# Softmax row sums inverted through 32x32 transposes, and one exponential of 128x1024 for both heads of a tile

## The chip, the cores and the metric

The kernel runs on one core of a Trainium2 chip. The metric is the device time of one execution in microseconds (us). A core has TensorE (PE in the profile; its weight loads are PEld), VectorE (DVE), ScalarE (ACT), GpSimd (POOL) and SyncE (SP, which only issues transfers here). Each engine runs its own instructions in order; they meet at semaphores.

## The reference

An image batch x of shape (8, 512, 32, 32) is group-normalised. A small gate (mean over the pixels, two layers, a sigmoid, a threshold) sends each channel to one of two branches. Both branches are multi-head self-attention over the 1024 pixels ("tokens") with 512 channels and 8 heads of 64. The first ("hyperbolic") branch scales every token before and after by functions of its norm. The result is x + branch 1 + branch 2. Cut to what the change touches, for each image and branch:

```
scores = einsum('bhnd,bhmd->bhnm', q, k) / sqrt(64)
attn = softmax(scores, axis=-1)
out = einsum('bhnm,bhmd->bhnd', attn, v)
out = out @ w_o + b_o
```

All data is float32. The softmax is computed here as exp(score - maximum), multiplied with v, and the product is multiplied at the end with 1 / (sum of the exponentials).

## The kernel before

The loops run over 8 images `i` and the 2 branches `t`, so there are 16 stages of some 239 us. A stage has 32 batches `b`, each of two score tiles. A score tile `g` holds 128 keys against 512 queries (half `h` of the tokens) for the two heads of a pair `p`; the heads lie in the two halves of the 128 partitions. `ph = 2p + h` counts the eight phases of a stage, each of 8 tiles (4 batches). The last stage of the last image is called "closing" in the code: nothing follows it, so work for the next image is left out.

TensorE (L1355 to L1536) works in a fixed order written out by hand. In a batch it makes the score tiles `scores(2b)`, `scores(2b+1)` (L1431, matmul L1449: a pair of matmuls, one for each head, in each of four terms), two tiles of scores of which only the maximum is wanted (`max_slot`, L1406, matmul L1413), the products with v of tiles already exponentiated (`prob_v`, L1454, matmul L1463), now and then the row sums (`denominator`, L1468, matmul L1477 with a matrix of ones), and a share of the next projections (`halves`, L1358, matmul L1364). At the end of a stage it projects the heads' outputs (`o_tile`, also L1364).

ScalarE exponentiates (`exps`, L854 to L872): for tile `g` it waits for a free slot of `probs`, then makes one ACTIVATE of 128x512 for each of the two heads. The input is one PSUM bank of `score_ps` per head (4 banks, so two tiles fit), the output one half of a slot of `probs` (4 slots of 128x1024). GpSimd adds up the eight `probs` tiles of a phase into `sums` (`probs_sum`, L681, L690) and later multiplies the output of a phase with the inverted sums (`mult`, L692, L697). ScalarE copies the row sums from PSUM to `den` (`den_copy`, L879).

VectorE takes the maximum of every `max_slot` tile out of PSUM (`max_slot`, L1194, L1201: it gives TensorE back the two banks, 0 and 1, that the next `max_slot` matmul needs), combines and turns the maxima (L1211, and eight transposes of 32x128 at L1224), makes the low parts of q, k and o (L1190, L1290), scales the next image's input (`scale_x`, L1101), computes the scales of the tokens (`x_root`, `x_blend` and the like, L975 to L995), and inverts the row sums (`recip`, L1281, L1285). All 64 rows of `den` that belong to one head are equal, since they come from a product with ones. Each phase's `den` of 128x512 is inverted in two parts of 256 columns, 6 and 8 batches after the phase's start; that of the last phase of a stage goes in one part of 512, behind the first output tile (L1345).

Of the kernel before, what the change touches and what calls it, by code (L numbers as in the profile page):

```python
# [8 lines left out]
ACT = mybir.ActivationFunctionType  # L9
# [4 lines left out]
P = 128  # L14
HALF = 512
# [3 lines left out]
PAIRS = HEADS // 2  # L19
HIDDEN = 128  # L20
GROUP = C // 32
SCALE = float(HD) ** -0.5
GN_EPS = 1e-5
EPS = 1e-5
SLOTS_P = 4
SCORE_BANKS, AUX_BANKS = 4, 3
# [36 lines left out]
BLOCK = 32  # L63
# [23 lines left out]
RECIP, RECIP_PARTS = [6, 8], 4  # L87
# [141 lines left out]
def build(nc, x, w1, b1, w2, b2, hw_qkv, hb_qkv, hw_o, hb_o, ew_qkv, eb_qkv, ew_o, eb_o, out):  # L229
    ctx = ExitStack()  # L230
    with ctx:
        ctx.enter_context(nc.allow_non_contiguous_dma(reason="biases, once"))

        def sb(name, shape, dt=F32):
            return ctx.enter_context(nc.sbuf_tensor(name, shape, dt))
# [25 lines left out]
        probs = sb("probs", [P, SLOTS_P, 2 * HALF])  # L261
# [4 lines left out]
        den = sb("den", [P, 2, HALF])  # L266

        mxw = sb("mxw", [P, 2, NT // 2, BLOCK], F32R)
        mxp = sb("mxp", [P, 2, NT, 2])
        group_mean = sb("group_mean", [P, P])  # L270
        ones = sb("ones", [P, HD])
        stats = sb("stats", [P, KC, 2, 6])
# [16 lines left out]
        score_ps = pb("score_ps", [P, SCORE_BANKS, HALF])  # L289
# [20 lines left out]
        def counted(name, per, before=0):  # L310
            return Count(sem(name), per, before)
# [16 lines left out]
                 for q in range(XIN)]  # L328
# [16 lines left out]
        c_free = {e: counted(n, frees(AUX, e), frees(FIRST, e))  # L345
                  for e, n in (("A", "aux_read_by_scalar"), ("D", "aux_read_by_vector"),
                               ("Q", "qk_lo_made"))}
        c_hi = counted("qk_hi_made", 32, 8)
        c_mx = counted("max_made", 16, 2)

        c_turn = [counted(f"max_rows_made{h}", 8, 1 - h) for h in range(2)]
        c_neg = [counted(f"max_rows_rounded{h}", 8, 1 - h) for h in range(2)]
        c_score = counted("scores_made", NSC)
        c_exp = counted("probs_made", NSC)
        c_pv = counted("probs_multiplied", 2 * TILES)
        c_sum = [counted(f"probs_summed{h}", NSUM) for h in range(2)]
        c_raw = counted("o_drained", 16)
        c_rec = counted("recip_made", 16 * RECIP_PARTS)
        c_on = counted("o_normal", 16)
        c_ohi = counted("o_hi_made", 16)  # L360
        c_olo = counted("o_lo_made", 16)
# [4 lines left out]
        c_dstep = counted("vector_step", DVE_STEPS, DVE_FIRST)  # L366
        c_astep = counted("scalar_step", ACT_STEPS, ACT_FIRST)
        COUNTS = [*c_wqk, c_wv, c_wo, *c_xin, c_xfree, c_ss, c_yread, c_ysc, c_ysm, c_xlo, c_xm, c_xg, c_keep, c_xa, c_pe_in, c_d2a, c_a2d, c_yd2a, c_ya2d, c_aux,
                  *c_free.values(), c_hi, c_mx, *c_turn, *c_neg, c_score, c_exp, c_pv, *c_sum, c_raw, c_rec, c_on, c_ohi, c_olo, c_sq,
                  c_sqf, *c_x, *c_vst, c_dstep, c_astep]  # L370

        def bank(name):
# [54 lines left out]
        def token_half(h):  # L427
            return slice(h * HALF, (h + 1) * HALF)
# [300 lines left out]
        def _(act):  # L729
# [120 lines left out]
            for i in range(B):  # L850
                steps[0] = 0
                for t in range(2):

                    def exps(g):  # L854
                        n = TILES * t + g
                        if n < SLOTS_P:

                            act.wait_ge(s_wlo, max(m + 1 for m in range(len(SPLITS)) if m % RAW_SLOTS == n))
                        if t and SLOTS_P - 2 <= g < SLOTS_P:

                            act.wait_ge(c_sqf.sem, c_sqf.at(i, 8))
                        last = max(n - SLOTS_P, -1)
                        act.wait_ge(c_pv.sem, c_pv.at(i, last + 1))
                        if last >= 0:
                            act.wait_ge(c_sum[(last // 8) % 2].sem,
                                        c_sum[(last // 8) % 2].at(i, (NT - 1) * (last // 16) + max(last % 8, 1)))
                        else:
                            act.wait_ge(c_sum[1].sem, c_sum[1].at(i, 0))
                        for u in (2 * n, 2 * n + 1):
                            act.wait_ge(c_score.sem, c_score.at(i, u + 1))  # L870
                            act.activation(probs[:, n % SLOTS_P, token_half(u % 2)], score_ps[:, u % SCORE_BANKS, :],  # L871
                                           ACT.Exp, scale=SCALE).then_inc(c_exp.sem, 1)  # L872

                    def drain(ph):
                        act.wait_ge(c_pv.sem, c_pv.at(i, TILES * t + 8 * ph + 8))
# [89 lines left out]
        def _(dve):  # L965
# [311 lines left out]
            for i in range(B):  # L1277
                steps[0] = 0
                for t in range(2):

                    def recip(ph, parts):  # L1281
                        n = 8 * t + ph
                        aux_read(dve, i, (t, "den", ph))
                        first, last = (parts[k] * HALF // RECIP_PARTS for k in (0, 1))
                        dve.reciprocal(den[:, ph % 2, first:last], den[:, ph % 2, first:last]).then_inc(c_rec.sem, parts[1] - parts[0])  # L1285

                    def o_lo(ph):
                        p, h = ph // 2, ph % 2
                        dve.wait_ge(c_ohi.sem, c_ohi.at(i, 8 * t + ph + 1))
                        dve.scalar_tensor_tensor(o_t[:, 1, p, token_half(h)], o_raw[:, ph % 2, :],  # L1290
                                                 bias_q[:, t, 2, p:p + 1], o_t[:, 0, p, token_half(h)].bitcast(F32),
                                                 ALU.add, ALU.subtract).then_inc(c_olo.sem, 1)

                    def lows(b):
                        for f in projections(b):
                            if f[0] == "qk" and wanted(i, t, f[1]):
                                qk_lo(i, t, f[1], f[2])

                    def y_done(k, t):
                        if t:  # L1300
                            ps = aux_made(dve, i, (1, "o", k))
                            dve.wait_ge(c_yread.sem, c_yread.at(i, k + 1))
                            dve.scalar_tensor_tensor(v_y[:, k, :], ps, bias_o[:, 1, k % KC:k % KC + 1], v_y[:, k, :],
                                                     ALU.add, ALU.add).then_inc(c_free["D"].sem, 1)
                        else:
                            dve.wait_ge(c_sq.sem, c_sq.at(i, k + 1))
                            dve.tensor_reduce(ss_y[:, k * ROWS:(k + 1) * ROWS], rows(y_square(k)), AX.X,
                                              ALU.add).then_inc(c_sqf.sem, 1)

                    for b in range(BATCHES):  # L1310
                        if t == 0 and b - 1 in GATE_BATCH and followed(i):
                            gate_read(i, t, GATE_BATCH[b - 1])
                        for j in range(2):
                            p, s = max_slot_at(b, j)
                            if wanted(i, t, p):
                                max_slot(i, t, p, s)
                                if s in HALF_DONE:
                                    combine(i, t, p, HALF_DONE.index(s))
                            if j == 0:
                                if t and b == Y_LAST:  # L1320
                                    y_done(7, 0)
                                if phase_at(b, LOW) is not None:
                                    o_lo(phase_at(b, LOW))
                                if t:
                                    y_scale_step(i, b)
                                    operand_step(i, t, b)
                                else:
                                    gate_step(i, b)
                                if b:
                                    lows(b - 1)  # L1330
                        for ph, parts in recips(b):
                            recip(ph, parts)
                        if t:
                            operand_tail(i, t, b)
                        else:
                            gate_tail(i, t, b)
                        if turn_at(b, TURN_AT) and wanted(i, t, turn_at(b, TURN_AT)[0]):
                            turn(i, t, *turn_at(b, TURN_AT))
                    o_lo(2 * PAIRS - 3)
                    lows(BATCHES - 1)  # L1340
                    o_lo(2 * PAIRS - 2)
                    lows(BATCHES)
                    if not closing(i, t):
                        y_done(0, t)
                    recip(2 * PAIRS - 1, (0, RECIP_PARTS))  # L1345
                    if closing(i, t):
                        y_done(0, t)
                    y_done(1, t)
                    o_lo(2 * PAIRS - 1)
                    for k in range(2, 8 if t else 7):  # L1350
                        y_done(k, t)
                assert steps[0] == DVE_STEPS or not followed(i), ("DVE_STEPS", steps[0])
# [210 lines left out]
```

## Time and profile before

| | |
|---|---|
| median of 3 runs | 3894.97 us (3889.81 to 3895.17) |
| the profiled execution | 3897.88 us |
| its span, first to last instruction | 3896.1 us |
| granted TensorE clock | 0.998 |
| busy: PE, PEld | 3827.4 us, 2396.8 us |
| busy: DVE, ACT, POOL | 2651.4, 1917.2, 2664.5 us |

Busy time is the union of an engine's instructions. The ends of matmuls are modelled and overlap the next one, so a short wait of PE can be hidden in its busy time; the distance from one start to the next shows it. In a row of the trace a number in brackets is the idle time of that engine before it and what ended it.

### The profile page before, as it was taken

The numbers are of one execution on the slowest core, as the hardware profiler recorded it, in microseconds if no ns is written. First come the engines' busy times: TensorE is split into PE (matmuls) and PEld (weight loads), VectorE is DVE, ScalarE is ACT, GpSimd is POOL, SyncE is SP. The second block draws the span as 40 slices with busy tenths as digits, with TensorE's granted clock in tenths as the row PEclk, the third lists the DMA queues.
The fourth block names the chain that finished last, engine by engine and source line by source line (L and its number), as shares of the span: only waits on it lengthen the run. The fifth ranks groups of instructions, "written<-read, shape, count | busy, mean of one in ns | idle before, by whom it ended". The sixth has DMA issues, their size and how long they took to land.

```text
span 3896.1 us, 57425 instructions
## 1 busy us (share of the span) xinstructions
PE 3827.4 (98%) x21164; PEld 2396.8 (62%) x21164; DVE 2651.4 (68%) x3576; ACT 1917.2 (49%) x3489; POOL 2664.5 (68%) x1300
## 2 busy tenths in 40 slices
PE   5999999999999999999999999999999999999999
PEld 3656566565665656566565665656656565565655
DVE  6675856758667585676857668576785758847566
ACT  4455534545345553555535555354553545535444
POOL 4584876838668486774867658675586856858468
PEclk9999999999999999999999999999999999999999
DMA  8212132121321213212141121411213112121102
GB/s 286 103 44 98 33 98 82 44 98 33 101 79 50 98 33 112 73 49 91 35 146 45 50 82 33 146 47 52 76 49 130 49 49 76 57 95 44 66 12 66
DMA packets 137555, 293.14 MB, mean 75 GB/s; under 512 B 16704, under 2 KB 28992, under 8 KB 127296
## 3 DMA queue, kind: packets, MB, share of 16 engines
q1 hardware_dynamic: 137280, 289.47, 21.9%
q8 instruction: 173, 2.83, 0.3%
q14 instruction: 102, 0.84, 0.1%
HBM read 239.09 MB, written 50.33 MB: 74 GB/s over the span
## 4 chain that ended last, share of the span: by engine, by line
PE 93%; DVE 4%; POOL 1%; issue 1%; DMA 0%; ACT 0%; SPq 0%; POOLq 0%; DVEq 0%; ACTq 0%
PE aux_ps L1364 32%; PE score_ps L1449 22%; PE acc_ps L1463 22%; PE aux_ps L1413 8%; PE score_ps L1364 4%; PE aux_ps L1477 3%; DVE mxp L1201 2%; POOL sums L690 1%; DVE neg_max L1224 0%; DVE xin L1101 0%; DMA w_split<-w_o 0%; DVE sc L995 0%; PE aux_ps L1379 0%; PE aux_ps L1382 0%; DVE den L1285 0%
## 5 line engine op out<-in xcount | busy, mean ns | idle before, releaser
L690 POOL TENSOR_TENSOR sums<-sums,probs 128x1024 f32<-128x1024 f32 x765 | 1832.8, 2396 | 723.3 <-ACT probs L871 668.9
L1201 DVE TENSOR_REDUCE mxp<-aux_ps 128x2 f32<-128x1024 f32 x1014 | 1240.3, 1223 | 884.6 <-PE aux_ps L1413 874.5
L871 ACT ACTIVATE probs<-score_ps 128x512 f32<-128x512 f32 x2048 | 1059.7, 603 | 1001.8 <-PE score_ps L1449 730.0
L1463 PE MATMUL acc_ps<-probs,v_y 128*64 128x512 f32 x4096 | 955.3, 599 | 0.6 <-ACT probs L871 0.6
L1364 PE MATMUL aux_ps<-xs,w_qk 128*128 128x512 f32 x2976 | 753.4, 401 | 0.0
L1364 PEld LDWEIGHTS aux_ps<-xs,w_qk 128*128 128x128 f32 x2976 | 537.8, 188 | 195.2 <-issue 89.4
L1463 PEld LDWEIGHTS acc_ps<-probs,v_y 128*64 128x64 f32 x4096 | 270.3, 136 | 529.7 <-issue 388.7
L690 POOL TENSOR_TENSOR sums<-probs 128x1024 f32<-128x1024 f32 x128 | 306.4, 2393 | 339.6 <-ACT probs L871 339.2
L1413 PE MATMUL aux_ps<-k_hi,q_hi 64*128 64x512 f32 x2028 | 459.8, 446 | 20.2 <-DVE mxp L1201 17.9
L1285 DVE RECIPROCAL den<-den 128x256 f32<-128x256 f32 (+1 forms) x240 | 443.9, 1850 | 14.7 <-ACT den L882 13.3
L1449 PE MATMUL score_ps<-q_hi,k_hi 64*128 64x512 f32 x2048 | 409.7, 393 | 0.6 <-ACT q_max L811 0.6
L1449 PE MATMUL score_ps<-q_hi,k_lo 64*128 64x512 f32 x2048 | 407.8, 391 | 0.0
L1449 PE MATMUL score_ps<-q_lo,k_hi 64*128 64x512 f32 x2048 | 406.3, 390 | 0.0
L1449 PE MATMUL score_ps<-q_max,first_rows 64*128 64x512 f32 x2048 | 405.0, 388 | 0.0
L1413 PEld LDWEIGHTS aux_ps<-k_hi,q_hi 64*128 64x128 f32 x2028 | 194.7, 183 | 340.2 <-issue 276.3
L1364 PE MATMUL aux_ps<-o_t,w_o 128*128 128x512 f32 x1536 | 355.4, 390 | 0.0
L1364 PEld LDWEIGHTS aux_ps<-o_t,w_o 128*128 128x128 f32 x1536 | 287.1, 188 | 72.1 <-issue 13.0
L1224 DVE STREAM_TRANSPOSE neg_max<-mxw 32x128 f32<-32x128 f32 x1024 | 308.7, 301 | 12.4
L697 POOL TENSOR_TENSOR o_raw<-o_raw,den 128x512 f32<-128x512 f32 x128 | 171.0, 1337 | 110.5 <-DVE den L1285 110.5
L1449 PEld LDWEIGHTS score_ps<-q_lo,k_hi 64*128 64x128 f32 x2048 | 196.5, 184 | 41.5
L1449 PEld LDWEIGHTS score_ps<-q_max,first_rows 64*128 64x128 f32 x2048 | 195.8, 184 | 42.1
L1449 PEld LDWEIGHTS score_ps<-q_hi,k_lo 64*128 64x128 f32 x2048 | 195.3, 184 | 39.5
(139 smaller groups left out, 3193.3 us busy)
## 6 DMA issues: line engine op xcount, KB each, us to landing
w_qk<-w_split SPq DMA_DIRECT2D x124, 512.0 KB, 4.2
xin<-in_x_dram SPq DMA_DIRECT2D x232, 256.0 KB, 3.4
w_o<-w_split SPq DMA_DIRECT2D x32, 1024.0 KB, 8.1
w_v<-w_split SPq DMA_DIRECT2D x30, 1024.0 KB, 7.8
v_y<-in_x_dram SPq DMA_DIRECT2D x72, 256.0 KB, 3.2
y<-v_y SPq DMA_DIRECT2D x64, 256.0 KB, 2.0
xin<-y SPq DMA_DIRECT2D x64, 256.0 KB, 3.2
out_dram<-v_y SPq DMA_DIRECT2D x64, 256.0 KB, 6.5
```

Of the source, the lines that this page charges most:

```text
L690: pool.tensor_tensor(sums[h][:, :], a, probs[:, g % SLOTS_P, :], ALU.add).then_inc(c_sum[h].sem, 1)
L697: pool.tensor_tensor(o_raw[:, ph % 2, :], o_raw[:, ph % 2, :], den[:, ph % 2, :], ALU.mult).then_inc(c_on.sem, 1)
L871: act.activation(probs[:, n % SLOTS_P, token_half(u % 2)], score_ps[:, u % SCORE_BANKS, :], ACT.Exp, scale=SCALE).then_inc(c_exp.sem, 1)
L1201: dve.tensor_reduce(mxp[:, :, n, h], ps, AX.X, ALU.max).then_inc(c_free["D"].sem, 1)
L1224: made = dve.transpose(rows[at:at + BLOCK, :, BLOCK * a:BLOCK * (a + 1)], mxw[BLOCK * a:BLOCK * (a + 1), j, :, :].bitcast(F32))
L1285: dve.reciprocal(den[:, ph % 2, first:last], den[:, ph % 2, first:last]).then_inc(c_rec.sem, parts[1] - parts[0])
L1364: last = nc.tensor.matmul(ps, lhs(a, k), rhs(b, k), start=(j == 0), stop=(j == len(todo) - 1))
L1413: last = nc.tensor.matmul(ps[:, j, :], q_hi[head(j), p % 2, n * P:(n + 1) * P], k_hi[head(j), p % 2, token_half(h)], start=True, stop=True)
L1449: last = nc.tensor.matmul(score_ps[:, (2 * n + j) % SCORE_BANKS, :], lhs, qq[head(j), cols] if qq is q_max else qq[head(j), p % 2, cols], ...
L1463: last = nc.tensor.matmul(acc_ps[head(j), :], v_y[:, m, head(2 * p + j)], probs[:, n % SLOTS_P, token_half(j)], start=(m == 0), stop=(m == ...
L1477: last = nc.tensor.matmul(ps[head(j), :], ones[:, :], term[:, token_half(j)], start=(n == 0), stop=(n == len(terms) - 1))
```

## The change

Inversion: a part of 256 columns of `den` is transposed in blocks of 32x32 into `den_cols` (a block's rows being equal, column 0 of each transposed block holds its 32 values, one per partition); the 8 such columns are inverted by one RECIPROCAL of 128x8 into `den_inv`; a second transpose reads each of the 8 values 32 times (a broadcast) and writes the inverted rows back to `den`. VectorE waits for each of the first two steps by a semaphore of its own. The last phase of a stage is now inverted in two parts of 256 instead of one of 512. Exponential: one ACTIVATE reads both banks of a tile and writes a whole slot; it waits for both heads' scores and adds 2 to the semaphore at its end.

```
-                        for u in (2 * n, 2 * n + 1):
-                            act.wait_ge(c_score.sem, c_score.at(i, u + 1))
-                            act.activation(probs[:, n % SLOTS_P, token_half(u % 2)], score_ps[:, u % SCORE_BANKS, :],
-                                           ACT.Exp, scale=SCALE).then_inc(c_exp.sem, 1)
+                        first = 2 * n % SCORE_BANKS
+                        act.wait_ge(c_score.sem, c_score.at(i, 2 * n + 2))
+                        act.activation(probs[:, n % SLOTS_P, :].rearrange("p (j q) -> p j q", j=2), score_ps[:, first:first + 2, :],
+                                       ACT.Exp, scale=SCALE).then_inc(c_exp.sem, 2)
...
-                        dve.reciprocal(den[:, ph % 2, first:last], den[:, ph % 2, first:last]).then_inc(c_rec.sem, parts[1] - parts[0])
+                        done, count = c_rec.at(i, RECIP_PARTS * n + parts[1]) - c_rec.at(i, 0), parts[1] - parts[0]
+                        cols = den[:, ph % 2, first:last]
+                        dve.transpose(den_cols[:, :, :].rearrange("p a c -> p (a c)"), cols).then_inc(c_dcol.sem, count)
+                        dve.wait_ge(c_dcol.sem, c_dcol.at(i, done))
+                        dve.reciprocal(den_inv[:, :], den_cols[:, :, 0]).then_inc(c_dinv.sem, count)
+                        dve.wait_ge(c_dinv.sem, c_dinv.at(i, done))
+                        dve.transpose(cols.rearrange("p (a c) -> p a c", c=BLOCK),
+                                      den_inv[:, :].unsqueeze(2).to_broadcast([P, HALF // BLOCK // 2, BLOCK])).then_inc(c_rec.sem, count)
...
-                    recip(2 * PAIRS - 1, (0, RECIP_PARTS))
+                    recip(2 * PAIRS - 1, (0, 2))
+                    recip(2 * PAIRS - 1, (2, 4))
```

## Rows read from the trace of the kernel before

**Rows 1.** The page's busy times: us, share of the span, instructions.
```profile
PE 3827.4 (98%) x21164; PEld 2396.8 (62%) x21164; DVE 2651.4 (68%) x3576; ACT 1917.2 (49%) x3489; POOL 2664.5 (68%) x1300
```
**Rows 2.** The first 95 us as a stretch: busy us (instructions) of each engine, PEclk, DMA.
```profile
0.00:95.00 95.00, 48.17 (x174) 34.35 (x175) 59.76 (x108) 42.62 (x60) 40.71 (x32) 0.91 0.84 293
```
**Rows 3.** PE's waits by releaser: us in total, times, longest.
```profile
PE aux_ps L1413 <- DVE mxp L1201: 17.9, 34, 1.4
```
**Rows 4.** The same view over all engines, VectorE's own largest wait.
```profile
DVE mxp L1201 <- PE aux_ps L1413: 874.5, 650, 10.6
```
**Rows 5.** Groups by line and shape: busy us, mean ns | idle before.
```profile
L1201 DVE TENSOR_REDUCE mxp<-aux_ps 128x2 f32<-128x1024 f32 x1014 | 1240.3, 1223 | 884.6 <-PE aux_ps L1413 874.5
L871 ACT ACTIVATE probs<-score_ps 128x512 f32<-128x512 f32 x2048 | 1059.7, 603 | 1001.8 <-PE score_ps L1449 730.0 <-POOL sums L690 271.1
L1463 PE MATMUL acc_ps<-probs,v_y 128*64 128x512 f32 x4096 | 955.3, 599 | 0.6 <-ACT probs L871 0.6
...
L1285 DVE RECIPROCAL den<-den 128x256 f32<-128x256 f32 x224 | 390.4, 1743 | 4.0 <-ACT den L882 2.6
...
L1224 DVE STREAM_TRANSPOSE neg_max<-mxw 32x128 f32<-32x128 f32 x1024 | 308.7, 301 | 12.4
...
L1285 DVE RECIPROCAL den<-den 128x512 f32<-128x512 f32 x16 | 53.6, 3348 | 10.7 <-ACT den L882 10.7
...
L824 ACT ACTIVATE o_t<-sums 128x1024 fp32r<-128x1024 f32 x4 | 4.1, 1052 | 6.2 <-DMA w_split<-o_t 6.2
```
**Rows 6.** Timeline of image 0, branch 1, batches 19 and 20: start, duration.
```profile
472.87 1.73 DVE L1285 RECIPROCAL den<-den 128x256 f32<-128x256 f32 x1
...
474.53 1.15 DVE L1201 TENSOR_REDUCE mxp<-aux_ps 128x2 f32<-128x1024 f32 x1
...
475.14 0.40 PE L1449 MATMUL score_ps<-q_max,first_rows 64*128 64x512 f32 x2
...
475.83 0.50 PE L1413 MATMUL aux_ps<-k_hi,q_hi 64*128 64x512 f32 x2 [0.30 <-DVE mxp L1201]
...
476.52 5.15 POOL L690 TENSOR_TENSOR sums<-sums,probs 128x1024 f32<-128x1024 f32 x2
...
477.60 1.84 DVE L1101 TENSOR_TENSOR xin<-xin,sc 128x512 f32<-128x512 f32 x1
...
479.37 2.51 DVE L1224 STREAM_TRANSPOSE neg_max<-mxw 32x128 f32<-32x128 f32 x8
...
482.66 0.39 PE L1449 MATMUL score_ps<-q_max,first_rows 64*128 64x512 f32 x2
...
483.28 0.50 PE L1413 MATMUL aux_ps<-k_hi,q_hi 64*128 64x512 f32 x2 [0.23 <-DVE mxp L1201]
```
**Rows 7.** Timeline around L995, batch 11 of branch 1, in images 0 and 2.
```profile
414.01 2.06 ACT L871 ACTIVATE probs<-score_ps 128x512 f32<-128x512 f32 x4 [0.74 <-PE score_ps L1449]
...
414.86 0.29 DVE L994 SCALAR_TENSOR_TENSOR sc<-ss,sc 128x128 f32<-128x128 f32 x1
...
415.18 4.86 POOL L690 TENSOR_TENSOR sums<-sums,probs 128x1024 f32<-128x1024 f32 x2 [0.50 <-ACT probs L871]
...
415.19 2.50 DVE L995 TENSOR_TENSOR sc<-sc 128x128 f32<-128x128 f32 x1
...
419.75 0.51 PE L1413 MATMUL aux_ps<-k_hi,q_hi 64*128 64x512 f32 x2 [1.11 <-DVE mxp L1201]
...
1372.84 0.29 DVE L995 TENSOR_TENSOR sc<-sc 128x128 f32<-128x128 f32 x1
...
1372.85 5.05 POOL L690 TENSOR_TENSOR sums<-sums,probs 128x1024 f32<-128x1024 f32 x2 [0.53 <-ACT probs L871]
```
**Rows 8.** PE's timeline at a stage's start, in the last stage and at its end.
```profile
332.96 0.50 PE L1413 MATMUL aux_ps<-k_hi,q_hi 64*128 64x512 f32 x2 [0.49 <-DVE mxp L1201]
...
3818.34 0.50 PE L1413 MATMUL aux_ps<-k_hi,q_hi 64*128 64x512 f32 x2 [0.42 <-DVE mxp L1201]
...
3870.53 22.05 PE L1364 MATMUL aux_ps<-o_t,w_o 128*128 128x512 f32 x96
```

More of the change, by code:

```diff
@@ L269, in build @@
         mxp = sb("mxp", [P, 2, NT, 2])
+        den_cols = sb("den_cols", [P, HALF // BLOCK // 2, BLOCK])
+        den_inv = sb("den_inv", [P, HALF // BLOCK // 2])
         group_mean = sb("group_mean", [P, P])
@@ L358, in build @@
         c_rec = counted("recip_made", 16 * RECIP_PARTS)
+        c_dcol = counted("den_columns_made", 16 * RECIP_PARTS)
+        c_dinv = counted("den_columns_inverted", 16 * RECIP_PARTS)
         c_on = counted("o_normal", 16)
@@ L368, in build @@
         COUNTS = [*c_wqk, c_wv, c_wo, *c_xin, c_xfree, c_ss, c_yread, c_ysc, c_ysm, c_xlo, c_xm, c_xg, c_keep, c_xa, c_pe_in, c_d2a, c_a2d, c_yd2a, c_ya2d, c_aux,
-                  *c_free.values(), c_hi, c_mx, *c_turn, *c_neg, c_score, c_exp, c_pv, *c_sum, c_raw, c_rec, c_on, c_ohi, c_olo, c_sq,
+                  *c_free.values(), c_hi, c_mx, *c_turn, *c_neg, c_score, c_exp, c_pv, *c_sum, c_raw, c_rec, c_dcol, c_dinv, c_on, c_ohi, c_olo, c_sq,
                   c_sqf, *c_x, *c_vst, c_dstep, c_astep]
```

## The prediction, made before the changed kernel was run

> **What bounds the kernel now.** I read the page's busy times first: TensorE is busy in 3827.4 us of a span of 3896.1 [rows 1], the others in half to two thirds. So I asked next for TensorE's own waits. Of its 68.7 us of idle time 46.8 lie in the first 95 us, before the loop over the images [rows 2], and the rest is nearly all one kind of wait: 17.9 us in 34 pieces (a few of them in the start-up) in which the next maximum-only matmul (L1413) wants its banks back from VectorE's reduce (L1201) [rows 3]. The products with v (L1463) waited for an exponential once, 0.6 us in 4096 matmuls [rows 5]. The other engines wait for TensorE: VectorE alone 874.5 us at the reduce [rows 4]. The change adds nothing to TensorE and takes nothing from it, so only those waits are to be had.
>
> I then looked up each of them in the timeline, by place:
> - Start of a stage, batch 0: the second maximum tile comes so soon that the reduce (1.2 us) is not done. The idle time is 0.49 us [rows 8], at 15 of the 16 stage starts (all but the first). No reciprocal and no exponential is in that chain.
> - Batch 11 of branch 1, in 4 of the 7 images: L995 takes 2.50 us instead of 0.29, since GpSimd's sum began 10 ns ahead of it; TensorE then idles 1.11 us. In the other 3 images L995 began 10 ns ahead of the sum and no time is lost [rows 7].
> - Batch 19 of branch 1, in all 8 images: a reciprocal of 1.73 us runs directly ahead of the reduce, and the next L1413 starts 0.69 us behind the last score matmul (475.14 to 475.83), where the pitch of a matmul is 22.05 / 96 = 0.23 us: 0.46 us lost [rows 6, 8]. The images differ: 0.46 in three of them, about 0.26 in four, and 0.58 in the last (idle 0.42 there [rows 8]); 3.0 us in all.
> - One batch later, in 7 images: 0.62 us from score to L1413 (482.66 to 483.28), 0.39 lost [rows 6], 2.7 us in all.
> - In the last stage the products wait 0.6 us for an exponential [rows 5].
>
> **The inversion.** Two reciprocals of known size give its rate: 3348 - 1743 ns for 256 more columns, 6.27 ns a column, so one of 8 columns takes 1743 - 248 x 6.27 = 188 ns [rows 5]. The transpose of 128 columns takes 301 ns on 32 partitions [rows 5]; one of 256 columns on 128 partitions isn't in the trace. Its bounds are 301 ns (size costs nothing) and 602 ns (all of it grows with the columns). I take the rate between the transpose and the reduce, (1223 - 301) / (1024 - 128) = 1.03 ns a column, which gives 301 + 132 = 433 ns. Two waits of VectorE for itself cost some 40 ns each, as between L994 and L995, 414.86 + 0.29 to 415.19 [rows 7]. A part is then 2 x 433 + 188 + 80 = 1.13 us, bounds 0.87 and 1.47, in place of 1.743: 0.61 us less. There are 224 parts of 256 and 16 of 512, thus 256 new parts; VectorE's busy time falls by 444 - 256 x 1.05, about 174 us. Nearly all of it lies beside TensorE, for VectorE has 874.5 us in which it only waits for it [rows 4]. GpSimd's multiply waits for the inverse (L697), but nobody on the path waits for that multiply except in the last phase of a stage, where four output tiles (48 matmuls of 0.23 us, 11 us [rows 8]) cover copy, reciprocal, multiply and split; the cover holds before and gets wider now.
>
> **Where the 0.61 us counts.** Only at batch 19. In the last image the reduce behind the reciprocal starts 0.6 us earlier and the 0.58 us go; nothing later in that stage takes them back, since the sums' chain starts from an exponential that comes earlier too. In the other seven images the gain is returned one batch later. The reduce ahead of 483.28 is late because of the turn at 479.37 (2.51 us), and that because `scale_x` (477.60, 1.84 us) stood behind a sum of GpSimd that began at 476.52 [rows 6]. The reciprocal is not in that chain: 0.61 us earlier, `scale_x` still meets the same sum, the turn still ends at 481.9, and TensorE, which arrives 0.46 us earlier, waits 0.46 us longer at 483.28. So: -0.6 us from the last image, 0 from the seven.
>
> **The exponential.** Two of 512 take 2.06 / 4 x 2 = 1.03 us of ScalarE in a row of four, and the first tile's pair ends some 1.09 us after its start (0.60 + 0.49; the pitch is (2.06 - 0.60) / 3, from 414.01 [rows 5, 7]). One of 1024 elements costs 1.05 us in the nearest row, a copy from SBUF [rows 5]; bounds 0.60 and 1.21. I take 1.03: the tile is ready 0.06 us earlier (bounds 0.49 earlier, 0.12 later). The wait for both heads costs nothing, as the two heads' last matmuls run side by side. TensorE's cover is wide: its products waited once. What the 0.06 us moves is GpSimd, which starts from exponentials, and through it `scale_x`: the seven stalls of batch 20 shrink by 0.06 us each, -0.4 us; and the wait in the last stage by 0.1.
>
> **The near-tie at L995.** Both sides move together. The sum at 415.18 starts 1.17 us after the exponential at 414.01; L995 stands behind the step L993, which was itself waiting for the end of GpSimd's sums ahead, and these also started from an exponential. Both come 0.06 us earlier, so I leave 4 collisions of 7. Each costs 1.2 us, so the tie is worth between -4.7 and +3.5 us.
>
> **A rule on the shared port.** In the trace no transpose was delayed by GpSimd: mean 301 ns over 1024 of them [rows 5], while L1101 and L995, with two inputs in SBUF, were [rows 6, 7]. The Trainium skill, SBUF — State Buffer, section Who interferes with whom, says that a VectorE instruction with one SBUF input contends with GpSimd only in a 2-port mode, and lists copy, cast and tensor_scalar as the ones that can enter it. By that rule the new transposes stay clear; were they in such a mode, the second rival below would hold.
>
> **The sum**, against the profiled execution: 3897.9 - 0.6 - 0.4 - 0.1 = 3896.8 us. The median of the runs is 2.9 us below the profiled execution, so I give 3894 us.
>
> **Rivals.**
> 1. *The tie falls well and the stalls stay gone.* GpSimd's phase is moved enough that L995 always wins, and batches 19 and 20 lose nothing: -4.7 - 2.4 - 2.7 beyond my sum, 3884 us. For it: the margins are 10 ns, and the lowest run shown, 3889.81, is 5 us below the others, about four collisions. Against it: the chain from 477.60 to the end of the turn holds no reciprocal. Half of it (about 3889 us) is likelier than all.
> 2. *The transposes queue behind GpSimd* (slower). Place: each part has two 128-partition, single-source SBUF transposes, and GpSimd is busy 68% of the time with sums of 2.4 us. A transpose that must wait would lose 0.68 x 1.2 = 0.8 us on average, a part 1.6 us, so it takes 2.7 us and not 1.74. The point from which it decides is a part longer than 1.74 us: at batch 19 every excess reaches TensorE at once, and elsewhere where VectorE had no idle time before the reduce (364 of 1014 reduces had none, [rows 4, 5]). 256 x 0.36 x 1.0 = 92 us: some 3985 us. Against it: the 301 ns of L1224.
> 3. *All seven images collide at L995*: +3.5 us, 3897.5; slower than before, but less than can be told.
> 4. *The wide ACTIVATE doesn't pay* (1.21 us, the crossing of two banks costing as much as a second instruction): no cover is used up, GpSimd starts 0.12 us later, +0.8 us in batch 20: 3895 us.
>
> **Chances.** My case with rival 4: 0.62; rival 3 and mixtures to that side: 0.15; rival 1 and its half: 0.18, of which 0.09 beyond the bound; rival 2 or another new contention of some size: 0.05. A change of 0.2% (7.8 us) is about what a measurement of this kernel can tell from none, so: faster 0.09, same 0.82, slower 0.09 (rival 2, and a part of rival 3 with further sums delayed). The range goes from 3887 (rival 1 almost whole) to 3902 (rival 3 with half a microsecond more in each stage).
>
> **What would show it.** L1285 must be of 128x8 near 190 ns and its transposes near 430 ns, none at 2 us; L871 1024 wide near 1.03 us, x1024; DVE's busy time down by some 170 us and ACT's by 20 to 60, with PE's busy time the same within a few us. PE's waits for mxp stay at some 16 us; the idle time at batch 19 is gone, that of batch 20 is larger by about as much; L995 shows 0.29 or 2.50. Transposes above 1 us, or products (L1463) that wait for exponentials, would make the prediction wrong; so would a PE busy time that falls by more than 5 us.

## The result: 0.18% slower, and the profile after

The changed kernel takes 3901.36 us (median of 20 runs, 3898.9 to 3903.48), the kernel before 3895.01 us (20 runs, 3889.81 to 3897.33): a ratio of 1.0018, 95% interval 1.0012 to 1.0024. The profiled execution takes 3902.38 us, its span is 3900.7.

The new instructions cost what was forecast. The page's busy times and the groups by line and shape of the changed kernel (columns as in [rows 1, 5]):

```profile
PE 3826.0 (98%) x21164; PEld 2397.8 (61%) x21164; DVE 2518.3 (65%) x4104; ACT 1859.9 (48%) x2465; POOL 2660.4 (68%) x1300
```

```profile
L877 ACT ACTIVATE probs<-score_ps 128x1024 f32<-128x1024 f32 x1024 | 999.3, 1024 | 1038.2 <-PE score_ps L1463 901.4 <-POOL sums L696 135.2 <-issue 0.5
...
L1303 DVE SCALAR_TENSOR_TENSOR o_t<-o_raw,bias_q,o_t 128x512 fp32r<-128x512 f32 x128 | 142.6, 1114 | 95.1 <-ACT o_t L893 95.1
L1297 DVE STREAM_TRANSPOSE den<-den_inv 128x256 f32<-128x256 f32 x256 | 114.0, 445 | 28.0 <-DVE den_inv L1295 1.4
L1293 DVE STREAM_TRANSPOSE den_cols<-den 128x256 f32<-128x256 f32 x256 | 110.9, 433 | 15.2 <-ACT den L888 14.0
...
L1107 DVE TENSOR_TENSOR xin<-xin,sc 128x512 f32<-128x512 f32 x56 | 86.6, 1557 | 0.7
...
L1295 DVE RECIPROCAL den_inv<-den_cols 128x8 f32<-128x8 f32 x256 | 52.3, 204 | 27.5 <-DVE den_cols L1293 1.4
```

For comparison, the two groups of the kernel before that the change doesn't touch and that moved all the same:

```profile
L1290 DVE SCALAR_TENSOR_TENSOR o_t<-o_raw,bias_q,o_t 128x512 fp32r<-128x512 f32 x128 | 127.9, 999 | 94.9 <-ACT o_t L887 94.9
L1101 DVE TENSOR_TENSOR xin<-xin,sc 128x512 f32<-128x512 f32 x56 | 65.5, 1180 | 0.7
```

Three things are to be seen. Transposes take 433 and 445 ns (forecast 433), the small reciprocal 204 (188), the wide exponential 1024 (1030). VectorE is busy 133 us less, ScalarE 57 us less, TensorE as before. And `scale_x` (L1107, before L1101) takes 1557 ns on average instead of 1180, the o low part (L1303, before L1290) 1114 instead of 999. Both have two inputs in SBUF.

TensorE's waits by releaser, answering to [rows 3] (us in total, times, longest):

```profile
PE aux_ps L1427 <- DVE mxp L1207: 20.1, 34, 1.9
...
PE aux_ps L1378 <- DVE o_t L1303: 3.4, 7, 0.5
```

The second row is new. Idle time understates these waits, as the last matmul's modelled end covers a part, so I measured from start to start of TensorE's instructions against the usual distance of each kind of step, and put every excess over 150 ns at its place. Places are counted in batches of branch 1, with the number of times over the images. "The blend" is the VectorE instruction at L995 (L1001 now), and a collision there is the case in which it takes 2.50 us instead of 0.29. A correction first: the two stalls that the prediction puts at "batch 19" and "batch 20" (and [rows 6] too) lie in batches 21 and 22 by the code (the `scale_x` with the turn behind it is the one of batch 21, the next that of batch 22).

| place, us lost (times) | before | after |
|---|---|---|
| batch 0, each stage but the first | 9.8 (15) | 9.7 (15) |
| batch 11, collision at the blend | 4.7 (4) | 0 |
| batch 21, behind the reciprocal | 3.1 (8) | 0 |
| batch 22, behind `scale_x` and the turn | 2.7 (7) | 5.5 (7) |
| batch 23 | 0 | 3.8 (7) |
| stage end, first output tile | 0 | 4.5 (7) |
| end of the last stage | 1.2 (2) | 1.2 (2) |

One more excess, 0.16 us before and 0.18 after, lies in batch 17 of one stage.

The sum of the changes is +3.3 us. The first score tile starts 1.1 us later (89.5 to 90.6 us), a difference of the start-up, where neither edit runs. Together 4.4, against 4.5 between the two profiled executions. Between the medians the loss is 6.35 us: the profiled execution before lay 2.9 us above its median, that of the changed kernel 1.0 above its own. The first may be its four collisions; no other execution of the kernel before has a trace, so that isn't shown.

**The stage end.** Timeline of image 0, branch 1, of the kernel before, and then of the changed kernel (start, duration):

```profile
538.46 1.74 DVE L1285 RECIPROCAL den<-den 128x256 f32<-128x256 f32 x1
...
540.28 1.64 POOL L697 TENSOR_TENSOR o_raw<-o_raw,den 128x512 f32<-128x512 f32 x1 [0.60 <-DVE den L1285]
...
545.12 0.75 DVE L1290 SCALAR_TENSOR_TENSOR o_t<-o_raw,bias_q,o_t 128x512 fp32r<-128x512 f32 x1 [4.35 <-ACT o_t L887]
545.37 1.66 POOL L709 TENSOR_TENSOR v_y<-v_y,xin 128x512 f32<-128x512 f32 x1
```

```profile
538.99 0.45 DVE L1297 STREAM_TRANSPOSE den<-den_inv 128x256 f32<-128x256 f32 x1
...
539.51 1.70 POOL L703 TENSOR_TENSOR o_raw<-o_raw,den 128x512 f32<-128x512 f32 x1 [0.17 <-DVE den L1297]
...
544.65 1.29 POOL L715 TENSOR_TENSOR v_y<-v_y,xin 128x512 f32<-128x512 f32 x1
544.80 1.69 DVE L1303 SCALAR_TENSOR_TENSOR o_t<-o_raw,bias_q,o_t 128x512 fp32r<-128x512 f32 x1 [4.74 <-ACT o_t L893]
...
546.63 3.00 PE L1378 MATMUL aux_ps<-o_t,w_o 128*128 128x512 f32 x12 [0.49 <-DVE o_t L1303]
```

GpSimd's multiply of phase 6 waited 0.60 us for the inverse; now it waits 0.17. All that follows on GpSimd (the last sum, the scaling of the residual, the residual sum L715) comes that much earlier. Before, the residual sum started 0.25 us behind VectorE's o low part; now it starts 0.15 us ahead of it, and the low part takes 1.69 us instead of 0.75. TensorE's first output tile needs it. It is the same in all seven images: the distance between the two starts is 234 to 250 ns on one side before, and 138 to 145 ns on the other after.

**Batches 21 to 23.** The timeline of image 0 in the changed kernel; the answering lines of before are [rows 6], and after them these two:

```profile
483.17 0.69 DVE L1101 TENSOR_TENSOR xin<-xin,sc 128x512 f32<-128x512 f32 x1
...
483.41 5.25 POOL L690 TENSOR_TENSOR sums<-sums,probs 128x1024 f32<-128x1024 f32 x2 [0.48 <-ACT probs L871]
```

```profile
474.38 0.43 PE L1427 MATMUL aux_ps<-k_hi,q_hi 64*128 64x512 f32 x2
...
475.43 5.15 POOL L696 TENSOR_TENSOR sums<-sums,probs 128x1024 f32<-128x1024 f32 x2
...
476.07 2.26 DVE L1107 TENSOR_TENSOR xin<-xin,sc 128x512 f32<-128x512 f32 x1
...
478.26 2.51 DVE L1230 STREAM_TRANSPOSE neg_max<-mxw 32x128 f32<-32x128 f32 x8
...
481.86 5.18 POOL L696 TENSOR_TENSOR sums<-sums,probs 128x1024 f32<-128x1024 f32 x2
482.06 2.74 DVE L1107 TENSOR_TENSOR xin<-xin,sc 128x512 f32<-128x512 f32 x1
482.17 0.50 PE L1427 MATMUL aux_ps<-k_hi,q_hi 64*128 64x512 f32 x2 [0.65 <-DVE mxp L1207]
...
486.08 0.50 PE L1427 MATMUL aux_ps<-k_hi,q_hi 64*128 64x512 f32 x2 [0.44 <-DVE mxp L1207]
```

The stall behind the reciprocal is gone (474.38), and comes back at 482.17, 0.81 us against 0.39, as forecast. What was not forecast: `scale_x` of batch 22 began 0.24 us ahead of GpSimd's next sum before (483.17 against 483.41) and begins 0.20 us behind it now. It is held for 2.1 us, and the reduce behind it is late for the matmul at 486.08. It begins behind the sum in all seven images, by 0.18 to 0.20 us in six of them and by 0.08 in image 1.

### The profile page after: what moved, and what is told of

Same layout as the page of the kernel before. It is cut to its first block, busy times and chain, and to the rows that moved or that the text cites. A ratio compares the mean times of both kernels' runs of the same rounds, so it can differ in the third digit from the quotient of the medians.

```text
span 3900.7 us, 58435 instructions
## 1 busy us (share of the span) xinstructions
PE 3826.0 (98%) x21164; PEld 2397.8 (61%) x21164; DVE 2518.3 (65%) x4104; ACT 1859.9 (48%) x2465; POOL 2660.4 (68%) x1300
## 4 chain that ended last, share of the span: by engine, by line
PE 92%; DVE 4%; POOL 1%; issue 1%; DMA 0%; ACT 0%; SPq 0%; DVEq 0%; POOLq 0%; ACTq 0%
PE aux_ps L1378 31%; PE score_ps L1463 23%; PE acc_ps L1477 22%; PE aux_ps L1427 8%; PE score_ps L1378 4%; PE aux_ps L1491 3%; DVE mxp L1207 2%; POOL sums L696 1%; DVE xin L1107 1%; DVE neg_max L1230 0%; DVE o_t L1303 0%; DMA w_split<-w_o 0%; PE aux_ps L1393 0%; PE aux_ps L1396 0%; DMA v_y<-in_x_dram 0%
## 5 line engine op out<-in xcount | busy, mean ns | idle before, releaser
L877 ACT ACTIVATE probs<-score_ps 128x1024 f32<-128x1024 f32 x1024 | 999.3, 1024 | 1038.2 <-PE score_ps L1463 901.4
L1463 PEld LDWEIGHTS score_ps<-q_hi,k_hi 64*128 64x128 f32 x2048 | 194.7, 185 | 34.8 <-issue 9.1
```

The costliest lines, as they stand in the source:

```text
L877: act.activation(probs[:, n % SLOTS_P, :].rearrange("p (j q) -> p j q", j=2), score_ps[:, first:first + 2, :], ACT.Exp, scale=SCALE).then_ ...
L1463: last = nc.tensor.matmul(score_ps[:, (2 * n + j) % SCORE_BANKS, :], lhs, qq[head(j), cols] if qq is q_max else qq[head(j), p % 2, cols], ...
```

## The experiments

Theory P (port order): the new instructions do no harm by their own time; the shorter inverse moves GpSimd's and TensorE's work by 0.4 us against VectorE's, and where a GpSimd instruction now begins ahead of a VectorE instruction with two SBUF inputs, VectorE is held for the rest of it. The rivals: the wide exponential does it (E), or the transposes and the two extra waits as such (T). Each comparison with the kernel before is between runs of one chip; the three groups (e1 to e4, e5 to e8, e9 to e11) ran on chips on which that kernel took 3894.8, 3891.1 and 3890.6 us. The changed kernel itself was not run again beside them. So a time set against its 3901.36 us compares two groups, and the ratio to the kernel before (1.0018 for the changed kernel) is the fairer measure; what settles a place is the trace. The sizes at each place are those of the one profiled execution of each kernel.

**One half at a time.** `e1_inverse_only` puts the old exponentials back:

```
-                        first = 2 * n % SCORE_BANKS
-                        act.wait_ge(c_score.sem, c_score.at(i, 2 * n + 2))
...
+                        for u in (2 * n, 2 * n + 1):
+                            act.wait_ge(c_score.sem, c_score.at(i, u + 1))
...
```

> The transposed inversion alone, with two exponentials of 128x512 as before. Theory P (port order): the shorter inverse lets GpSimd's multiply and sum of the last phase but one end 0.4 us earlier, so its residual sum reads SBUF ahead of the o low part and holds it back; TensorE waits 0.65 us at the first output tile of branch 1 in 7 images (4.6 us), and about 0.5 us in batch 23 (3.7 us) since TensorE, and with it the exponential, comes 0.4 us earlier at scale_x of batch 22. Time 3900 to 3902 us against 3895 of before. Rival E (the wide exponential): GpSimd's earlier start, 0.06 us with the wide instruction, is what tips the ties; then this kernel has neither wait and takes 3894 to 3896 us.

Measured: 3908.46 us (7 runs), before 3894.82; ratio 1.0031 (1.0020 to 1.0043). The loss is here, and by the medians it is larger than with both edits (the interval touches that of the changed kernel, which ends at 1.0024). Both new stalls are there: the stage end in all seven images (4.5 us), batch 23 in six (3.4), with 5.4 us at batch 22. Image 1 is a test that nobody set up: there `scale_x` of batch 22 starts 16 ns ahead of the sum and takes 0.69 us, and the stall of batch 23 is missing; in the other six it starts 131 to 173 ns behind and takes 2.78 to 2.81. Rival E falls, but my number was 6 us too low. The rest is at batch 11. Its timeline in image 0 of this kernel:

```profile
412.40 4.86 POOL L696 TENSOR_TENSOR sums<-sums,probs 128x1024 f32<-128x1024 f32 x2 [0.51 <-ACT probs L877]
412.41 2.51 DVE L1001 TENSOR_TENSOR sc<-sc 128x128 f32<-128x128 f32 x1
...
416.98 0.50 PE L1427 MATMUL aux_ps<-k_hi,q_hi 64*128 64x512 f32 x2 [1.11 <-DVE mxp L1207]
```

Five of seven images collide so in the profiled execution (3905.42 us; 5.9 us lost); with seven, 2.4 us more would be lost, of the 3 us that the median lies above it. No trace of such a run shows seven.

`e2_exp_only` puts the wide exponential alone into the kernel before (the first hunk of the change).

> The wide exponential alone, with the reciprocals of 128x256 as before. Theory P: no new waits; TensorE's waits are those of before, 0.3 to 0.5 us in batch 21 and 0.4 in batch 22; 3893 to 3896 us. Rival E: the whole loss is here, 3900 to 3902 us.

Measured: 3891.08 us (11 runs), before 3894.82; ratio 0.9990 (0.9981 to 0.9999). No new stall; no collision at the blend in the profiled execution (0 of 7, the sum's start 3 ns ahead to 16 ns behind L995's, which took 0.29 us each time). Batch 21 and 22 lose 2.3 and 2.8 us. So this edit does no harm, and rival E falls here too. It is 3.7 us faster than the kernel before on this chip and 2 us below the range that I had given; that this comes from fewer collisions fits their price, but no run here separates it.

**The instructions without their speed.** `e3_long_inverse` inverts 12 columns of each block, 11 of them for nothing:

```
-        den_inv = sb("den_inv", [P, HALF // BLOCK // 2])
+        den_inv = sb("den_inv", [P, HALF // BLOCK // 2, 12])
...
-                        dve.reciprocal(den_inv[:, :], den_cols[:, :, 0]).then_inc(c_dinv.sem, count)
+                        dve.reciprocal(den_inv[:, :, :], den_cols[:, :, 0:12]).then_inc(c_dinv.sem, count)
...
-                                      den_inv[:, :].unsqueeze(2).to_broadcast([P, HALF // BLOCK // 2, BLOCK])).then_inc(c_rec.sem, count)
+                                      den_inv[:, :, 0:1].to_broadcast([P, HALF // BLOCK // 2, BLOCK])).then_inc(c_rec.sem, count)
```

> The changed kernel, with the reciprocal between the transposes made 12 columns of each block instead of 1 (96 columns, about 0.74 us instead of 0.20), so that a part takes about 1.72 us again, as the plain reciprocal did (1.74). Theory P: the instructions are all there, but their time is the old one, so GpSimd and TensorE arrive as before; both new waits go and the old ones of batch 21 come back: 3894 to 3897 us. Rival T (the transposes themselves or the two extra waits on VectorE do the harm): 3901 us or more.

Measured: 3897.16 us (11 runs), 4.2 below the changed kernel; ratio to before 1.0005 (0.9996 to 1.0014). Three instructions, both extra waits, and the old duration; groups by line and the stage end of this kernel:

```profile
L1295 DVE RECIPROCAL den_inv<-den_cols 128x96 f32<-128x96 f32 x256 | 192.8, 753 | 27.5 <-DVE den_cols L1293 1.4
```

```profile
543.60 0.88 DVE L1303 SCALAR_TENSOR_TENSOR o_t<-o_raw,bias_q,o_t 128x512 fp32r<-128x512 f32 x1 [4.18 <-ACT o_t L893]
544.00 1.62 POOL L715 TENSOR_TENSOR v_y<-v_y,xin 128x512 f32<-128x512 f32 x1
```

The low part is first again, by 0.41 us in all seven images, and neither new stall occurs. Making VectorE's work longer by 0.55 us a part made the kernel faster; the intervals of the two ratios overlap a little (this one ends at 1.0014, that of the changed kernel begins at 1.0012), but the traces leave no doubt about the two places. Rival T falls. Six blends collide in the profiled execution (6.9 us, against 4.7 for four before), which fits a time at the upper end of the range.

**The order, put right by a wait.** `e4_low_before_sum` is the changed kernel with one wait on GpSimd ahead of the residual sum:

```
+                        if k == 0:
+                            pool.wait_ge(c_olo.sem, c_olo.at(i, 15))
                         pool.tensor_tensor(v_y[:, k, :], v_y[:, k, :], chunk, ALU.add).then_inc(c_yread.sem, 1)
```

> The changed kernel, with one wait more on GpSimd: its first residual sum of a stage (v_y + y) starts only after VectorE's o low part of the last phase but one. Theory P: TensorE's 0.65 us at the first output tile of branch 1 goes in all 7 images, 4.6 us: 3896 to 3898 us; the batch 23 wait stays. Rival: the wait of the output tile has another cause (ScalarE's copy, the multiply) and stays: 3901 us.

Measured: 3897.66 us (11 runs), 3.7 below the changed kernel; ratio to before 1.0007 (0.9999 to 1.0016). The stage end of this kernel:

```profile
544.52 0.75 DVE L1305 SCALAR_TENSOR_TENSOR o_t<-o_raw,bias_q,o_t 128x512 fp32r<-128x512 f32 x1 [4.73 <-ACT o_t L895]
...
545.44 1.29 POOL L717 TENSOR_TENSOR v_y<-v_y,xin 128x512 f32<-128x512 f32 x1 [1.14 <-DVE o_t L1305]
```

GpSimd waits 1.14 us and no wait of TensorE comes of it, and TensorE's wait at the first output tile is gone in all seven images, as expected; the one of batch 23 stays (in six images; in image 1 `scale_x` is 30 ns ahead, and it is missing). That the time fits as well is luck in part: three blends collide here (3.4 us) and none did in the changed kernel's profiled execution, while the first score tile starts 1.5 us earlier (89.1 against 90.6).

`e5_two_waits` adds the same for batch 22:

```
+                            if t and g == 44 and followed(i):
+                                pool.wait_ge(c_xg.sem, c_xg.at(i, 8))
```

> The changed kernel with the wait of e4_low_before_sum and a second one: GpSimd's first sum of batch 22 (branch 1) starts only after scale_x of that batch. Theory P (order on the port): scale_x takes 0.7 us instead of 2.7, the 0.5 us that TensorE waits at batch 23 go in all 7 images (3.8 us), beside the 4.6 us of the first wait: 3893 to 3895 us if the number of collisions at the blend (L1001) stays at 2 or 3 of 7. Rival (VectorE has too much to do between batches 22 and 23, in whatever order): the wait at batch 23 stays, 3897 to 3898 us.

Measured: 3889.61 us (11 runs) where the kernel before takes 3891.10; ratio 0.9998 (0.9990 to 1.0007). Batch 22 of image 0 in this kernel:

```profile
479.16 0.69 DVE L1111 TENSOR_TENSOR xin<-xin,sc 128x512 f32<-128x512 f32 x1
...
479.93 4.95 POOL L696 TENSOR_TENSOR sums<-sums,probs 128x1024 f32<-128x1024 f32 x2 [1.01 <-DVE xin L1111]
```

`scale_x` takes 0.69 us instead of 2.74 in all seven images, and batch 23 loses nothing. The profiled execution had no collision. The time is below the 3893 to 3895 us that I expected, with two or three collisions and on the level of the first group, where the kernel before took 3.7 us more. The interval of the ratio ends at 1.0007, below that of the changed kernel, which begins at 1.0012. Both new stalls of the change are now accounted for by the order alone.

`e6_four_waits` adds two more: the first sum of batch 11 waits for the blend, and that of batch 21 for its `scale_x`:

```
+                            if t and g == 22 and followed(i):
+                                pool.wait_ge(c_dstep.sem, c_dstep.at(i, 31))
+                            if t and g == 42 and followed(i):
+                                pool.wait_ge(c_xg.sem, c_xg.at(i, 7))
```

> The changed kernel with four such waits: also the first sum of batch 11 behind the blend, and the first sum of batch 21 behind scale_x of that batch. Theory P: no collision at the blend, and the 0.8 us of batch 22 go too (5.5 us): 3886 to 3889 us, faster than both kernels. Rival (GpSimd is full in batches 15 to 24, so a sum that starts 1.3 us later holds up exponentials): no better than the kernel with two waits, 3893 us or more.

Measured: 3893.82 us (11 runs), before 3891.10; ratio 1.0010 (1.0000 to 1.0019): a miss. The 5.5 us of batch 22 did go, but 10.0 us came in their place, in batch 24, all at one step. TensorE's waits in this kernel:

```profile
PE aux_ps L1386 <- POOL xs L670: 8.9, 7, 1.3
```

GpSimd is full there, as the rival said, only the victim is another one: not the exponentials but the last low part of x (`x_lo`, L670), which the projection of the next stage needs. `e7_exp_three_waits` is the wide exponential with the plain reciprocals and the waits of batches 11, 21 and 22.

> The wide exponential with the plain reciprocals and the three waits of batches 11, 21 and 22. Theory P: 0.4 us of batch 22 go (2.8 us), the wait behind the reciprocal in batch 21 (0.25 us in 7 images, 0.58 in the last, 2.3 us) stays, since the reciprocal itself makes it: 3887 to 3890 us, 2 us or so above the kernel with four waits; that difference is what the short inverse is worth once the order is fixed. Rival: no difference from the wide exponential alone, 3891 us.

Measured: 3897.72 us (11 runs), before 3891.10; ratio 1.0017 (1.0008 to 1.0026): a miss for the same reason, with 10.1 us at the same step. Its rival (3891 us) missed too. The difference between e6 and e7 (3.9 us) is partly batch 21, which loses 2.3 us here and nothing in e6; of the other part, 1.2 us is a later start of the first score tile, and the rest is not settled.

**The blend.** `e8_inverse_tie` is e1 with the wait of batch 11.

> The inversion alone with one wait: the first sum of batch 11 behind the blend. Theory P: with the inversion alone nearly all of the 7 images collide at the blend (5 of 7 in the profiled execution, and the median run is 3 us above that one, so probably all), at 1.18 us each; with the wait none does: 3908.5 - 8.3 = 3900 us, where the changed kernel is. Rival: the loss of the inversion alone against the changed kernel lies elsewhere (the narrow exponentials' own time): 3905 us or more.

Measured: 3900.90 us (8 runs), before 3891.10; ratio 1.0026 (1.0016 to 1.0036). No blend collides. The profiled executions of e1 and e8 differ by 3905.42 - 3899.27 = 6.15 us, and five collisions are 5.9. The other stalls are those of e1: 5.4, 3.3 and 4.5 us, with the one of batch 23 missing in image 1 again (`scale_x` 7 ns ahead of the sum). So the collisions are settled by the traces. That the median hits 3900 is luck in part: against the kernel before on the same chip the loss is 9.8 us, where it was 13.6 for e1, so the wait is worth 3.8 us by that measure and not 8.3.

`e10_before_tie` is the kernel before with that wait.

> The kernel before with one wait: the first sum of batch 11 behind the blend. Theory P: what sets a run of the kernel before at 3890 or at 3897 us is the number of collisions there (0 to 7, 1.18 us each); with the wait it is always 0: 3889 to 3891 us with a spread of under 2 us, whatever the chip. Rival: the spread has another source, and the median stays that of the kernel before.

Measured: 3889.94 us (3888.52 to 3892.17, 11 runs), before 3890.55 (3888.0 to 3893.48); ratio 0.9999 (0.9990 to 1.0008). The level is as expected, but the spread is 3.7 us and not under 2, and on this chip the kernel before is at that level without the wait. So it doesn't show that the collisions make the difference between 3890 and 3895 us from chip to chip; that fits their number and price but was only argued. A rival for the spread is the start-up: in the thirteen profiled executions of this document the first score tile starts between 87.1 and 90.6 us, 3.5 us apart.

**What is left.** `e9_three_waits` is the changed kernel with the waits of e5 and that of batch 11; `e11_exp_two_waits` the wide exponential alone with the waits of batches 11 and 22.

> The changed kernel with three waits on GpSimd: batch 11 (first sum behind the blend), batch 22 (first sum behind scale_x), stage end (residual sum behind the o low part); not that of batch 21, which held up the low parts of x. Theory P: as the kernel with two waits in its profiled execution, which had no collision at the blend: 3888 to 3890 us on either chip. Rival: the wait of batch 11 itself costs time, 3891 us or more.

> The wide exponential with the plain reciprocals and the waits of batches 11 and 22. What the short inverse is worth when the order on the port is fixed: it removes 0.25 us in 7 images and 0.58 in the last at batch 21 (2.3 us), and the 0.4 us at batch 22 grow to 0.8 in 7 images (2.8 us). Theory P: so this kernel and the changed one with three waits agree within 1 us, 3888 to 3891 us. Rival: the short inverse is worth its 2 us and more, this one is at 3892 us.

Measured: 3891.73 (3889.13 to 3893.33) and 3890.55 us (3889.34 to 3892.97), 11 runs each, before 3890.55; ratios 1.0002 (0.9993 to 1.0012) and 1.0001 (0.9992 to 1.0010). The first is above its range of 3888 to 3890, though in its profiled execution the places and sizes of the stalls are those of e5; its first score tile starts at 89.8 us and that of e5 at 87.7, so between these two executions most of the difference is in the start-up. The two kernels of this pair agree within 1.2 us (1 was expected): with the order fixed, the short inverse is worth nothing that can be measured, since it takes 2.3 us from batch 21 and gives 2.5 us to batch 22 (5.3 against 2.8). No version beats the kernel before by more than the measurement can tell.

## Why the prediction was wrong

- **What bounds the kernel**: right. TensorE's busy time moved by 1.4 us, and what was gained or lost is in waits at a few places, but for 1.1 us of start-up.
- **The costs of the new instructions**: right to 16 ns (reciprocal), 12 ns (second transpose) and 6 ns (exponential). VectorE's busy time fell by 133 us and not by 174: 21 us are `scale_x`, 15 the o low part, both held longer, and 8 the new instructions (256 parts of 1.08 us and not 1.05); the four collisions that are gone take 9 off again, so some 6 us are unexplained.
- **The gain at "batch 19", returned one batch later**: right. 3.1 us went (0.58 of it in the last image, which gave nothing back), 2.8 came back in the other seven.
- **The exponential's -0.4 and -0.1 us**: they didn't come, and nor did a loss. With the wide exponential alone (e2) batch 22 loses 2.8 us, as before (2.7), and the end of the last stage 1.3 (1.2).
- **The tie at L995**: I left 4 collisions of 7; there were none in the profiled execution of the changed kernel, 5 in e1, 3 in e4 and 6 in e3. I could not forecast a tie of 10 ns; its price was right (1.18 us each), and the range allowed for it.
- **The step that failed** is in the part on the inversion: "nobody on the path waits for that multiply except in the last phase of a stage", and with it that 174 us of shorter VectorE work cost nothing. Nobody waits for the multiply, but those behind it on GpSimd's queue come earlier, and one of them takes the port ahead of an instruction that TensorE does wait for. I asked who gains from a faster engine and not whom its followers now precede. e3 and e4 show it from both sides: the longer inverse, or a wait on GpSimd, removes the stall. The same omission stands behind "The reciprocal is not in that chain": that holds for the `scale_x` of batch 21, but I stopped there. TensorE arrives 0.4 us earlier, so do the exponential and the sum of batch 22, and the lead of 0.24 us that the next `scale_x` had was lost; e5 shows it. Together 8.3 us (4.5 and 3.8) that my sum had at nothing.
- **The rivals**: rival 2 (transposes queued behind GpSimd) is excluded by the rows: 433 and 445 ns on average, against at least 1 us. The Trainium skill, SBUF — State Buffer, section Who interferes with whom, says that a VectorE instruction with at most one SBUF input, outside the 2-port modes, doesn't contend with GpSimd, and that one with two SBUF inputs contends with a GpSimd instruction that reads SBUF. The trace agrees on both: of each kind of new transpose 226 of 256 began while GpSimd was in an instruction, and they took as long as the other 30 (medians 434 and 433 ns for the first, 445 and 445 for the second, none over 448), while `scale_x`, with two, went from 0.69 to 2.74 us. What happened is near what the chances call "a part of rival 3 with further sums delayed", turned round: further sums early. I gave slower 0.09 in all, and 6.35 us is inside the 0.2% that I called the same; with 20 runs of each kernel that bound was too wide, as the interval (1.0012 to 1.0024) shows.
- **The range** reached to 3902, so the median lay inside it, and that is luck in part: the four collisions that my sum kept didn't occur in the profiled execution, and with their 4.7 us that execution would have stood at 3907. Wrong was the sign: no change was forecast (3894 against 3895), and a loss clear of its interval was measured.

## What to carry to other kernels

Where two engines take turns at one port, look for the near-ties before changing a duration on either: here the leads were 0.25, 0.24 and 0.01 us, and a change of 0.4 us turned the first two round in every image. Shortening work that nobody waits for isn't free then; what follows it on its consumers' queues moves too. An order that holds only by such leads can be written down as a wait. Here two such waits took the loss back (e5), but none made the kernel faster than it was before the change, and one on an engine that was full at that place cost 10 us elsewhere (e6, e7).

## What the runs showed of the hardware

A 128x128 TENSOR_TENSOR of VectorE with both inputs in SBUF takes 0.29 us when it starts 10 ns ahead of a GpSimd sum, and 2.50 us when it starts 10 ns behind it [rows 7]; GpSimd's two sums then take 4.86 us, 2.4 each. The change from one to the other lies within a few ns: in these traces every blend that took 2.5 us started 5 ns or more behind the sum, and some up to 6 ns behind still took 0.29 (e5). The transposes between SBUF tensors ran beside GpSimd's instructions at 433 and 445 ns; 433 is what 301 ns for 128 columns on 32 partitions and 1.03 ns for each further column give. A reciprocal costs 6.2 ns a column down to 8 columns, and some 155 ns besides (204 ns at 8, 753 at 96, 1743 at 256). One ACTIVATE over two PSUM banks takes 1024 ns where two take 603 each and 1.09 us together.
